# One pass for the last key tile and for the corrections of a graph layer, with the first norm's rows written back and reloaded

## The reference

```
def _L0_gnn_ref(inst_feature, aggregator_matrix, rel_pair_index, Wq, bq, Wk, bk):
    q = (inst_feature[sub] @ Wq.T + bq).reshape(-1, HEADS, DK)      # sub, obj: the 10000 pairs
    k = (inst_feature[obj] @ Wk.T + bk).reshape(-1, HEADS, DK)
    att = ((q * k).sum(-1) / np.sqrt(DK)).T
    scores = jnp.zeros((HEADS, n, n)).at[:, sub, obj].set(att)
    scores = jnp.where((1.0 - aggregator_matrix).astype(bool)[None], -jnp.inf, scores)
    scores = scores.at[:, di, di].set(1e-07)
    attn = jax.nn.softmax(scores, axis=2)
    return (attn.sum(axis=0) / HEADS) @ inst_feature
def _L1_gnn_ref(x, adj, weight, bias):
    return jnp.matmul(adj, jnp.matmul(x, weight)) + bias
x = _layernorm(x + _L0_gnn_ref(...), axis=-1)
x = _layernorm(x + _L1_gnn_ref(...), axis=-1)
```

## Time and profile before

| what | value |
|---|---|
| median of three runs | 171.88 us |
| profiled execution, span (all that is given of its own time) | 217.5 us |
| PE busy over the span | 166.0 us, 1053 matmuls |
| DVE busy | 125.9 us |
| ACT busy | 75.2 us |
| POOL busy | 65.9 us |
| mean granted clock of TensorE | 0.885 of full speed |

### The profile page before, as it was taken

The page is one execution under the profiler, slowest core; times in us unless marked ns, Lnnn a source line. Parts: engine busy times, 40 slices in busy tenths (PEclk is TensorE's granted clock), DMA queues, the critical chain, the costliest instruction groups (busy, mean ns, idle before and its releaser), DMA issues.

```text
span 217.5 us, 2923 instructions
## 1 busy us (share of the span) xinstructions
PE 166.0 (76%) x1053; PEld 84.6 (39%) x1053; DVE 125.9 (58%) x389; ACT 75.2 (35%) x126; POOL 65.9 (30%) x80
## 2 busy tenths in 40 slices
PE   4999521100011899999999999999999998999990
PEld 4844100000000245554454444475446553444450
DVE  3865360000400487887998967796989321766572
ACT  6677061000110177533237516261421120323333
POOL 7777777777771000000006723340000000000000
PEclk9999955555555599999999999999999999999998
DMA  6999959000000075189102200600000000122114
GB/s 184 387 352 308 327 178 357 29 0 0 1 0 0 15 217 184 48 278 371 45 37 77 22 0 18 190 5 6 0 0 0 3 2 9 50 99 96 51 73 145
DMA packets 12999, 22.65 MB, mean 104 GB/s; under 512 B 4478, under 2 KB 5662, under 8 KB 12850
## 3 DMA queue, kind: packets, MB, share of 16 engines
q1 hardware_dynamic: 7570, 18.17, 24.5%
q10 hardware_dynamic: 3280, 3.07, 4.1%
q0 software_dynamic: 2128, 1.16, 2.3%
HBM read 16.70 MB, written 5.68 MB: 103 GB/s over the span
## 4 chain that ended last, share of the span: by engine, by line
PE 64%; issue 22%; DVE 6%; POOL 4%; DMA 2%; ACT 0%; DVEq 0%; POOLq 0%
PE acc L1313 17%; PE acc L1246 15%; PE acc L1397 10%; PE tr L1246 7%; POOL found L611 3%; PE tr L1227 3%; PE tr L1232 3%; PE tr L1397 2%; DMA found<-in_adj,top_i 2%; PE acc L1421 2%; PE tr L1352 1%; PE tr L1387 1%; DVE st L845 1%; DVE y L894 1%; DVE hot L864 1%
## 5 line engine op out<-in xcount | busy, mean ns | idle before, releaser
L1313 PE MATMUL acc<-adjT,x1s 128*128 128x512 f16 (+3 forms) x264 | 52.4, 354 | 0.0
L606 POOL DMA_INDIRECT ed_adj<-in_adj,ed_idx x47 | 46.5, 989 | 14.5 <-issue 14.0
L1246 PE MATMUL acc<-xs,adjT 128*128 128x512 f16 (+1 forms) x176 | 43.1, 393 | 7.2 <-issue 7.1
L1313 PEld LDWEIGHTS acc<-adjT,x1s 128*128 128x128 f16 (+1 forms) x264 | 25.0, 98 | 23.4 <-issue 0.6
L1246 PEld LDWEIGHTS acc<-xs,adjT 128*128 128x128 f16 (+1 forms) x176 | 16.8, 99 | 30.9 <-issue 13.9
L1232 PE MATMUL tr<-bit_eye,adjT 128*128 128x65 f16 x121 | 7.4, 196 | 26.9 <-issue 26.9
L611 POOL DMA_INDIRECT found<-in_adj,top_i x8 | 8.7, 1084 | 50.9 <-DVE top_i L927 48.8
L1397 PE MATMUL acc<-whl,xs 128*128 128x512 f16 (+1 forms) x108 | 23.8, 370 | 0.0
L1246 PE MATMUL tr<-xs,adjT 128*128 128x512 f16 (+1 forms) x66 | 16.8, 388 | 7.3 <-issue 7.3
L1232 PEld LDWEIGHTS tr<-bit_eye,adjT 128*128 128x128 f16 x121 | 5.7, 98 | 30.0 <-issue 26.3
L825 DVE COPY counts<-tr 128x1 f32<-128x1 f32 x11 | 1.5, 140 | 26.9 <-remote 26.9
(11 more groups left out here) (273 smaller groups left out, 232.6 us busy)
## 6 DMA issues: line engine op xcount, KB each, us to landing
stage<-in_adj_T SPq DMA_DIRECT2D x9, 704.0 KB
x_sb<-in_x SPq DMA_DIRECT2D x3, 768.0 KB, 7.3
sums_dram<-y ACTq DMA_DIRECT2D x6, 256.0 KB
sums_dram<-xd ACTq DMA_DIRECT2D x5, 256.0 KB, 3.1
out<-y SPq DMA_DIRECT2D x5, 256.0 KB, 2.0
stage<-in_adj_T SPq DMA_DIRECT2D x3, 384.0 KB, 3.7
hot<-row_dram SPq DMA_DIRECT2D x1, 1024.0 KB
stage<-in_L_gnn_weight SPq DMA_DIRECT2D x1, 1024.0 KB, 5.3
```

The source lines that it names most:

```text
L606: nc.gpsimd.indirect_dma_start(out=ed_adj[0:EP, c:c + 1], out_offset=None, in_=adj_flat, in_offset=bass.IndirectOffsetOnAxis(ap=ed_idx[0:E ...
L1246: last = mm(sum_bank(i)[:, :], adjT[0:width[k], k, i * P:(i + 1) * P], xs[0:width[k], half, k, :], start=(k == 0 and half == 0), stop=(k = ...
L1313: ins = mm(mix_bank(u)[:, 0:j - i], x1s[0:width[k], half, k, f * P:(f + 1) * P], adjT[0:width[k], k, i:j], start=(k == 0 and half == 0), s ...
```

## The change

The change has six parts.

1. **Last key tile in one pass.** The 74 rows of the last key tile are split into 64 (`EVEN`) and 10 (`ODD`). Two small copies lay the high part of the 64 rows on partitions 0 to 63 and the low part on 64 to 127 (`x1_tail`), with `adj` twice beside them (`adj_tail`), so that one matmul a unit takes the place of two. PE waits for these copies (`tail_laid`) at row 20.
2. **The odd 10 rows as slots.** They are put into slots 53 to 62 (`x1_odd`, added to `dx1`), so that the correction carries them. The limit of live pairs is now 53 (`CAP`).
3. **One-pass corrections.** `stackL` holds the slots' columns twice, `stackR` the high part of the change times the weight in its upper half and the low part in its lower. `correct` is one matmul.
4. **x1 written back and reloaded.** What `stackR`'s lower half did before (the change in x1) is done through memory: SP stores each x1 tile as it is ready, POOL scatters the new rows of the slots into it, and SP loads all of x1 again in four parts before the out phase. DVE waits for these parts at output tiles 0, 1, 5 and 6.
5. **Around it:** the product with the weight has 128 stationary columns instead of 64, ACT and DVE write the split change twice, POOL copies the gathered columns twice (53 rows each, 63 once before) and gathers 128 rows of them instead of 63. DVE's one-hot (L1040) goes; two small instructions and one of 64x512 come.
6. **Rows.** The slot chain's small products stand 1 to 5 rows later in `MIX_ORDER`.

```diff
+EVEN = 64
+ODD = LAST - EVEN
+CAP = BIAS_ROW - ODD
+BACK_PARTS = ((0, 1), (1, 5), (T - 1, T), (5, T - 1))
+BACK_BEFORE = {0: 0, 1: 1, 5: 2, 6: 3}
...
             sp.dma_start(wT[:, 1], wk_t.rearrange("(k p) o -> p k o", p=P)).then_inc(wk_loaded, 16)
+            for half in range(2):
+                sp.dma_start(adj_tail[EVEN * half:EVEN * half + EVEN, 0:N], adjT[0:EVEN, T - 1, 0:N]).then_inc(tail_laid, 16)
+            for t in range(T):
+                sp.wait_ge(x1_ready, t + 1)
+                sp.dma_start(rows(x1_dram, t), x_sb[0:width[t], t, :]).then_inc(x1_stored, 16)
+            sp.wait_ge(x1_hi, T)
+            sp.dma_start(x1_tail[0:EVEN, :], x1s[0:EVEN, 0, T - 1, :]).then_inc(tail_laid, 16)
+            sp.wait_ge(x1_lo, T)
+            sp.dma_start(x1_tail[EVEN:P, :], x1s[0:EVEN, 1, T - 1, :]).then_inc(tail_laid, 16)
...
+            sp.wait_ge(x1_scattered, 16)
+            for n, (a, b) in enumerate(BACK_PARTS):
+                if b < T:
+                    sp.dma_start(x_sb[:, a:b, :], x1_dram[a * P:b * P, :].rearrange("(t p) h -> p t h", p=P)).then_inc(x1_back[n], 16)
...
+            pool.wait_ge(adj_cast, T - 2)
+            nc.gpsimd.memset(x1_odd, 0.0).then_inc(odd_zeroed, 1)
...
-            nc.gpsimd.tensor_copy(stackL[0:BIAS_ROW, 0:N], col_rows).then_inc(cols_laid, 1)
-            pool.wait_ge(cols_laid, 1)
+            nc.gpsimd.tensor_copy(stackL[0:CAP, 0:N], col_rows[0:CAP]).then_inc(cols_laid, 1)
+            nc.gpsimd.tensor_copy(stackL[SLOTS:SLOTS + CAP, 0:N], col_rows[SLOTS:SLOTS + CAP]).then_inc(cols_laid, 1)
+            pool.wait_ge(cols_laid, 2)
+            pool.wait_ge(back_ready, 1)
+            pool.wait_ge(row_ready, 1)
+            pool.wait_ge(x1_stored, 16 * T)
+            nc.gpsimd.indirect_dma_start(
+                out=x1_dram, out_offset=bass.IndirectOffsetOnAxis(ap=back_i[:, 0:1], axis=0),
+                in_=q[0:SLOTS, :], in_offset=None, bounds_check=N - 1, oob_is_err=False).then_inc(x1_scattered, 16)
...
-            nc.scalar.mul(dT[:, 0, :], tr[0][:, 0:KF * SLOTS], XS).then_inc(dT_hi, 1)
-            act.wait_ge(change_ready, 1)
-            nc.scalar.mul(stackR[64:P, 0, :], dx1[64:P, :], WS).then_inc(right_hi, 1)
+            nc.scalar.mul(dT[:, 0], twice(tr[0]), XS).then_inc(dT_hi, 1)
             act.wait_ge(dS_done, 1)
-            nc.scalar.mul(stackR[0:BIAS_ROW, 0, :], tr[2][0:BIAS_ROW, :], 1.0 / XS).then_inc(right_hi, 1)
+            for at in (SLOTS, 0):
+                nc.scalar.mul(stackR[at:at + BIAS_ROW, :], tr[2][at:at + BIAS_ROW, :], 1.0 / XS).then_inc(right_hi, 1)
...
-            V.tensor_scalar(stackL[64:P, :], col_no[64:P, :], sub[64:P], None, ALU.is_equal).then_inc(low_ready, 1)
...
+            dve.wait_ge(odd_in, 16)
+            step(V.tensor_scalar(x1_odd, x1_odd, fits[0:SLOTS], None, ALU.mult))
...
-            step(V.tensor_scalar(q, q, norm_b[:, 8:9], norm_b[:, 9:10], ALU.mult, ALU.add))
-            step(V.tensor_tensor(dx1, q, kk, ALU.subtract))
-            V.tensor_scalar(dx1, dx1, rep, None, ALU.mult).then_inc(change_ready, 1)
+            V.tensor_scalar(q, q, norm_b[:, 8:9], norm_b[:, 9:10], ALU.mult, ALU.add).then_inc(row_ready, 1)
+            dve.wait_ge(row_ready, 1)
+            step(V.tensor_tensor(dx1[0:SLOTS], q[0:SLOTS], kk[0:SLOTS], ALU.subtract))
+            V.scalar_tensor_tensor(dx1[0:SLOTS], dx1[0:SLOTS], rep[0:SLOTS], x1_odd, ALU.mult, ALU.add).then_inc(change_ready, 1)
...
+                if t in BACK_BEFORE:
+                    dve.wait_ge(x1_back[BACK_BEFORE[t]], 16)
...
-                    for half in range(2):
-                        ins = mm(mix_bank(u)[:, 0:j - i], x1s[0:width[k], half, k, f * P:(f + 1) * P], adjT[0:width[k], k, i:j],
-                                 start=(k == 0 and half == 0), stop=(k == T - 1 and half == 1))
...
+                    if k < T - 1:
+                        for half in range(2):
+                            mm(mix_bank(u)[:, 0:j - i], x1s[:, half, k, f * P:(f + 1) * P], adjT[:, k, i:j],
+                               start=(k == 0 and half == 0), stop=False)
+                    else:
+                        pe.wait_ge(tail_laid, 16 * 4)
+                        mm(mix_bank(u)[:, 0:j - i], x1_tail[:, f * P:(f + 1) * P], adj_tail[:, i:j],
+                           start=False, stop=True).then_inc(mix_done, 1)
...
-                for half in range(2):
-                    last = mm(bank, stackL[:, t * P:(t + 1) * P], stackR[:, half, columns], start=False, stop=(half == 1))
-                last.then_inc(out_done, 1)
+                mm(bank, stackL[:, t * P:(t + 1) * P], stackR[:, columns], start=False, stop=True).then_inc(out_done, 1)
```

More of the change, by code:

```diff
@@ L105, in resnorm_graph @@
         table = sb("table", [P, P], f16)
-        stackR = sb("stackR", [P, 2, H], f16)
+        stackR = sb("stackR", [P, H], f16)
+        adj_tail = sb("adj_tail", [P, NP], f16)
+        free = KF * H + N
+        x1_odd = flat_stage[0:SLOTS, free:free + H]
+        x1_tail = flat_stage[:, free + H:free + H + H // 2].bitcast(f16)
+        back_i = sb("back_i", [SLOTS, 1], i32)
         ident = sb("ident", [P, P])
@@ L402, in general_dve @@
                 dve.wait_ge(y_stored[b], 16 * len(range(b, T, YS)))
+            for part in x1_back:
+                dve.wait_ge(part, 16)
             step(V.tensor_scalar(pos_all, ed_ok[0:EP], -float(N * N), float(N * N), ALU.mult, ALU.add))
@@ L509, in y4, with twice @@
             return (y if t % 4 < 2 else xd)[:, t % 2, :]
+        def twice(bank):
+            return bank[:, 0:KF * SLOTS].rearrange("p (k s) -> p k s", k=KF).unsqueeze(2).broadcast_to([P, KF, 2, SLOTS])
         def edge_slice(n):
@@ L711, in _ @@
             act.wait_ge(late_consts, 4)
-            nc.scalar.activation(stackL[0:64, :], col_no[0:64, :], ACT.Identity, bias=ones[0:64, 0:1], scale=0.0).then_inc(ones_laid, 1)
+            nc.scalar.activation(stackL[:, :], col_no[:, :], ACT.Identity, bias=ones[:, 0:1], scale=0.0).then_inc(ones_laid, 1)
             mix_high(3)
@@ L1057, in _ @@
             step(V.scalar_tensor_tensor(keep, dup_key, 0.0, valid, ALU.is_equal, ALU.mult))
+            step(V.tensor_scalar(slot[0:SLOTS, 10:11], rep[0:SLOTS], -FAR, FAR, ALU.mult, ALU.add))
+            V.tensor_tensor(back_i[:, :], slot[0:SLOTS, 10:11], slot[0:SLOTS, 0:1], ALU.add).then_inc(back_ready, 1)
             dve.wait_ge(bias_split, 1)
@@ L1171, in _ @@
             dve.wait_ge(dT_hi, 1)
-            V.scalar_tensor_tensor(dT[:, 1, :], tr[0][:, 0:KF * SLOTS], XS, dT[:, 0, :], ALU.mult, ALU.subtract).then_inc(dT_lo, 1)
+            for two in range(2):
+                V.scalar_tensor_tensor(dT[:, 1, :, two], tr[0][:, 0:KF * SLOTS].rearrange("p (k s) -> p k s", k=KF), XS, dT[:, 0, :, two],
+                                       ALU.mult, ALU.subtract).then_inc(dT_lo, 1)
             dve.wait_ge(right_hi, 1)
-            V.scalar_tensor_tensor(stackR[64:P, 1, :], dx1[64:P, :], WS, stackR[64:P, 0, :], ALU.mult, ALU.subtract).then_inc(right_lo, 1)
-            dve.wait_ge(right_hi, 2)
-            V.scalar_tensor_tensor(stackR[0:BIAS_ROW, 1, :], tr[2][0:BIAS_ROW, :], 1.0 / XS, stackR[0:BIAS_ROW, 0, :],
-                                   ALU.mult, ALU.subtract).then_inc(right_lo, 1)
+            low = slice(SLOTS, SLOTS + BIAS_ROW)
+            V.scalar_tensor_tensor(stackR[low, :], tr[2][low, :], 1.0 / XS, stackR[low, :], ALU.mult, ALU.subtract).then_inc(right_lo, 1)
             mix_low(10)
@@ L1386, in _ @@
                 for n, (a, b) in enumerate(((0, 0), (0, 1), (1, 0))):
-                    last = mm(tr[2][0:64, :], dT[:, a, k * SLOTS:(k + 1) * SLOTS], whl[:, b, k, :],
+                    last = mm(tr[2][:, :], dT[:, a, k].rearrange("p two s -> p (two s)"), whl[:, b, k, :],
                               start=(k == 0 and n == 0), stop=(k == KF - 1 and n == 2))
             last.then_inc(dS_done, 1)
-            mix_rows(122, UNITS * T)
+            mix_rows(127, UNITS * T)
             def weigh(bank, n, columns):
```

66 lines of the change are left out of this document (39 added, 27 removed).

## The result

The changed kernel is slower: 174.33 us median of 4 runs (173.29 to 176.63) against 171.8 of the kernel before, a ratio of 1.014 (95% interval 1.009 to 1.019). Four more runs beside a later series gave 174.4 to 177.1; of all eight the median is 175.3. The forecast was 168.4. The ratio is taken from the undisturbed runs alone, which leaves out the slowest, 176.63 us, and that is the run profiled here; the second profile (experiment 9) is of a run of 175.33 us.

A forecast was written before the change was run, and what follows sets the result against it. PE's matmuls were taken to bound the kernel, with DVE's slot chain just in time behind them. 4.46 us saved, less waits of 0.6, 0.1, 0.1 and 0.15, gave -3.5 us: 171.88 to 168.4 us, range 167.0 to 170.5.

The forecast's parts named there:

- what PE is rid of: PE's matmuls: 2.30 us less from the last key tile's one pass, 2.16 from one-pass corrections, 4.46 us in all.
- the sum: All terms added: -4.46 + 0.6 + 0.1 + 0.1 + 0.15 = -3.5 us; by stages 97.9 us from the second product's start.
- the wait at `mixed`: PE arrives earlier at `mixed` while DVE's chain is unchanged: 0.6 us wait (bounds 0 and 0.7); rival without it 0.10.
- The transposes of the change and dS: After `mixed`: transposes 0.4 us spare; PE waits 0.1 us (bounds 0 and 0.3) for the split change, written twice.
- POOL's copies: POOL's second copy of gathered columns: cost 0, as the gather lands late and DVE's L1069 goes first.
- the 0.7 us on PE: Case of an early gather: L1069 is held for both copies and PE waits 0.7 us at the dots.
- scatter and reload: Write-back before the out phase: scatter lands by 172.7, reload parts by 178.0 to 183.2, first two 3.6 and 4.0 us spare.
- The slower rival: Late scatter: taking 13.8 us, it makes DVE's first output tile wait 5.1 us, 173.5 us in all; chance 0.06.
- The copied tail: PE at row 20 waits for the copies, landing 3.8 us after issue: 0.1 us, range 0 to 0.7.
- The branch: PE's halt of 0.99 us at the branch grows by 0.15 us with the reload under way, bounds 0 and 1.5.
- a rival, with a chance of 0.09: The branch's halt and DVE's first reads fall into the reload: halt 2.5 instead of 0.99 us, 169.9 us; chance 0.09.
- the idle row: Profile row before the change: PE halts 0.99 us at the branch with no load or store under way.

The follow-up runs named there:

- experiment 9: The changed kernel run again with no edit: median 176.2 us of 4 runs (174.4 to 177.1), profiled run 175.33 us.
- experiment 6: The changed kernel with the tail written straight into the stack and the reload's fourth part issued only after the two early look-ups are read: 169.24 us, ratio 0.983.
- experiment 4: The changed kernel with 13 matmuls into a free bank ahead of row 20, so PE doesn't idle there: 173.95 us, ratio 1.016.
- experiment 5: The changed kernel with the last key tile written straight into the stack by ScalarE and VectorE, no copies: 173.59 us, ratio 1.013.
- experiment 2: The changed kernel with the reload's fourth part issued only after PE read the two look-ups ahead of the branch: 171.03 us median.
- experiment 8: The kernel before, with two 1 MB loads that nothing reads put on SP's queue ahead of the branch: 176.93 us, ratio 1.029.
- experiment 1: The changed kernel with the last key tile's 64 rows again in two passes, read where they lie, no copies: 172.44 us, ratio 1.003.

## Why the prediction was wrong

*Right: what PE is rid of, 4.46 us.* `mixed` to the weighing fell by 1.77 us, and at full clock (experiment 6) the stage from the first to the last correction by 2.30, output tiles 2.81 us apart. Experiment 6, with both losses away, needs 98.1 us from the start of the second product where the sum had 97.9.

*Right: the wait at `mixed`.* 0.6 was forecast, 0.5 came. The transposes of the change and dS did not wait, where 0.1 was set.

*Right in cost, not in its reason: POOL's copies.* The forecast had the gather land late and L1123 (L1069 before) go first in 0.7 us. It landed after 6.0 us, 1.0 more than before as its bytes had it, but still ahead of L1121's end, and L1123 took 1.80 us beside the first copy, like the earlier trace rows:

```profile
98.29 2.28 DVE L1121 SCALAR_TENSOR_TENSOR whl<-stage,whl 128x2048 f16<-128x2048 f32 x1
100.49 1.80 DVE L1123 SCALAR_TENSOR_TENSOR xo<-wraw,xo 64x512 f16<-64x512 f32 x1
102.21 1.11 DVE L1129 SCALAR_TENSOR_TENSOR wraw<-tr,bias_q,wraw 128x128 f32<-128x128 f32 x4
```

The copies took 1.59 and 1.66 us at 100.15 and 101.80. L1121 ended at 100.57 and L1123 at 102.29, and a copy ended 1.17 us behind either of them, the 1.2 us that the prediction gave to one copy. So L1123 was held by the first copy alone, and the second was held by L1123; the prediction had L1123 held by both. L1129 was not held. PE's dots waited for nothing. The Trainium skill, SBUF — State Buffer, Who interferes with whom, agrees for L1123, held in full; the 0.7 us on PE that the prediction drew from its rule did not come.

*Right: scatter and reload.* The scatter landed in 4.2 us, the parts of the reload in 2.5, 6.1 and 12.3, and VectorE waited for none of them. The slower rival was out. (By the prediction's own terms the branch came at 180.9 and VectorE's first read at 182.4, not 180.5 and 181.6; that only adds to the slack.) But the reload was judged only by who waits for its data.

*Wrong: "The copied tail", +0.1, upper end 0.7.* The landing was taken as 3.8 us from a 2 KB transfer on an idle queue, with 0.6 for the stores ahead of it. It was 4.5 and 5.0 in the median, 5.8 for the second copy of the first profile, and PE waited 1.7 and 2.6 us. Two things were left out. Behind the 2.6 us the half clock follows, 1.5 us more (experiment 4). And without the copies the look-ups bind, so that the flags come at +14.6 to +15.0 (experiments 5 and 6), 0.7 to 1.1 us later than the sum had them. The stage costs +1.4 us in the second profile and +3.9 in the first.

*Wrong: "The branch", +0.15, bounds 0 and 1.5; this step decides the sign.* The halt is 4.0 to 4.3 us instead of 0.99, and the half clock behind it takes 1.7 to 2.7 us more. Together 4.7 to 6.0, which is more than all of the 4.46. The text had the right mechanism as a rival, with a chance of 0.09, and named that halt and reload overlap nearly for certain. The failure was to take the idle row as the nearest one for a branch that would no longer be idle, to cap the rival at 2.5 us with no row behind that figure, and to let nothing follow it.
The Trainium skill, Runtime: NRT & Kernel Launch, Instruction fetch mechanics, says that a taken branch to a far target waits for a DMA fetch of its page. That it also grows with traffic is what experiments 2, 6 and 8 show. Here it was the rule to follow.

*The ledger* of the first profile against before, from the table: flags +3.9, `mixed` to weighing -1.8, halt +3.0, corrections -0.6 (2.3 gained, 1.7 lost to the clock), end +0.2: +4.7 us. For the second profile it is +1.4 - 1.8 + 3.3 + 0.45 + 0.2 = +3.6. The two profiled runs were 4.8 and 3.7 us over the medians of before in their series; the medians differ by 2.5 in the first series and 4.6 in the second.

*Open:* why the second copy lands after 4.9 us in one execution and 5.8 in another. The halt is long because an instruction packet starts late, while what follows the packet takes 2.6 to 3.1 us with traffic and without. That the packet stands behind the reload's packets until then is argued from this and from the full DMA engines; the profile doesn't show when it was asked for.

## What to carry to other kernels

A transfer that is added off the critical path has to be laid against everything that uses the DMA engines at that time, not only against who reads its data: an engine's instruction fetch behind a branch is such a user, and the profile lists it only as a packet of an instruction queue in the DMA view. When the forecast has TensorE idle for microseconds, price the matmuls behind the wait at half clock too. And before a wait is shortened, look up which one ends next behind it: here the look-ups stood 0.3 to 0.7 us ahead of the copy (+14.6 to +15.0 against +15.28) and kept most of what its removal could give.

## What the runs showed of the hardware

- The halt at the branch: 0.4 us with no write-back at all, 0.8 to 1.0 with the queues nearly idle, 1.7 at the tail of a reload, 2.6 to 4.3 in the middle of one, 3.4 with two loads of 1 MB in the kernel before. In the long ones PE went on some 2 to 3 us after the DMA share had fallen. In all 13 profiles it went on 2.6 to 3.1 us after a 16 KB instruction packet started (2.58 before the change, 2.98 in the first profile after it).
- The clock: behind a PE idle of 1.5 us (experiment 5), 1.6 (2) and 1.7 (1 and 9) it stayed at 2.4 GHz; behind 2.6 (twice), 3.4, 3.7, 4.0 and 4.3 us (twice) it was 1.2 GHz. Coming back cost 1.5 to 2.7 us over the matmuls behind the idle, and this differs between executions of one kernel.
- A copy of 64 KB inside SBUF from issue to landing, median of the two: 3.7 us without x1's stores, 4.0 with the last store behind it in the queue (one profile each), 4.5 to 5.0 with it ahead (four).
- VectorE and GpSimd: an instruction of VectorE with two inputs in SBUF, 512 columns wide, took 1.80 us beside a GpSimd copy, where another of that width took 0.68, and the copies of 53x1354 ended 1.17 us behind the VectorE instruction that each met.
- A 64-row matmul between 128-row ones costs 0.05 us more than its columns; the 74-row ones of the kernel before were in a stretch of 62 matmuls at 0.216 us each and show no such price.
